# Second self-attention of a gated decoder kernel: fetch groups of four tiles, nine tiles ahead, with key products and weighted adds placed anew

## The reference, cut to what matters

```python
for l in range(L):                                   # L = 2
    x = x + _attn(_ln(x, ln1_w[l], ln1_b[l]), wq[l], wk[l], wv[l], wo[l], ...)   # 16 heads of 8, causal
    h = _ln(x, ln2_w[l], ln2_b[l])
    moe = _token_moe if l % 2 == 0 else _seq_moe
    x = x + moe(h, gate_w[l], gate_b[l], e_w1[l], e_b1[l], e_w2[l], e_b2[l])
# _token_moe: out = sum over 8 experts of _ffn(h, expert e) * cw[..., e], two of the cw are not zero (top 2)
# _ln: (x - mean) / sqrt(var + 1e-05) * w + b
```

## Time and profile before

| what | value |
|---|---|
| median of three runs | 1240.01 us |
| the profiled execution | 1244.81 us |
| its span, first to last instruction | 1243.1 us |
| PE busy | 1000.3 us (80%) |
| DVE busy | 834.7 us (67%) |
| ACT busy | 723.2 us (58%) |
| POOL busy | 587.8 us (47%) |
| mean granted TensorE clock | 0.857 |
| POOL's key products L658 (all three attentions) | x192, 242.4 us busy, 1284 ns each |
| DVE's maximum L1471 and subtraction L1474 | x96 each, 1215 and 1225 ns each |

### The profile page before, as it was taken

One profiled execution on the slowest core, in us unless ns is written; L12 is line 12 of the kernel. 1 busy time (PEld: TensorE's weight loads), 2 busy tenths in 40 slices (PEclk: granted clock), 3 DMA queues, 4 the chain that ended last, 5 costly groups with the idle time before them and its releaser, 6 DMA issues.

```text
span 1243.1 us, 30490 instructions
## 1 busy us (share of the span) xinstructions
PE 1000.3 (80%) x9835; PEld 772.5 (62%) x9835; DVE 834.7 (67%) x1980; ACT 723.2 (58%) x1821; POOL 587.8 (47%) x804
## 2 busy tenths in 40 slices
PE   4999988999974899996068799965999989899503
PEld 2677766677664899996036666754777769455301
DVE  4599998899866656664348897767222245499873
ACT  2577777878831077775055678843555532688543
POOL 6355545555640145553776765612334310478433
PEclk9899999999975599998577899965999995699855
DMA  4000040000011022222110004000000002011002
GB/s 126 11 15 15 15 140 2 2 1 0 1 39 29 11 58 63 67 64 50 52 27 20 20 8 135 1 1 0 1 0 0 0 19 59 11 45 46 27 0 68
DMA packets 51922, 38.77 MB, mean 31 GB/s; under 512 B 6073, under 2 KB 45477, under 8 KB 51861
## 3 DMA queue, kind: packets, MB, share of 16 engines
q1 hardware_dynamic: 46956, 28.88, 8.0%
q0 software_dynamic: 4320, 8.86, 2.8%
q10 hardware_dynamic: 584, 0.26, 0.1%
HBM read 29.13 MB, written 8.85 MB: 31 GB/s over the span
## 4 chain that ended last, share of the span: by engine, by line
PE 49%; DVE 14%; issue 11%; ACT 10%; POOLq 7%; POOL 3%; DMA 2%; SPq 1%; another core or an unknown queue 1%; DVEq 1%; ACTq 0%
PE ps_s L1036 9%; PE ps_o L1036 9%; PE ps_t L1120 7%; PE ps_v L1036 6%; PE ps_t L1036 6%; PE ps_a L1036 5%; POOLq L713 4%; ACT work L836 2%; POOL work L714 2%; DVE inner_all L1666 2%; PE ps_v L1140 1%; POOLq L703 1%; ACT vst L827 1%; DVE rowmax L1471 1%
## 5 line engine op out<-in xcount | busy, mean ns | idle before, releaser
L658 POOL TENSOR_TENSOR kbd<-kts,kmask 128x512 f32<-128x512 f32 x192 | 242.4, 1284 | 210.5 <-ACT qts L822 128.0
L844 ACT COPY probs_t<-ps_t 128x1024 f32<-128x1024 f32 x96 | 97.2, 1013 | 72.8 <-PE ps_t L1120 71.8
L678 POOL DMA_INDIRECT xg<-x_rows,row_from x71 | 73.8, 1039 | 137.6 <-DVE slot_of L1636 70.1
L1471 DVE TENSOR_REDUCE rowmax<-ps_s 128x16 f32<-128x1024 f32 x96 | 116.7, 1215 | 30.7 <-PE ps_s L1036 30.6
L1036 PE MATMUL ps_s<-kbd,qts 64*64 64x512 f32 (+1 forms) x1024 | 127.7, 571 | 0.2 <-issue 0.2
L1474 DVE TENSOR_TENSOR work<-ps_s,rowmax 128x1024 f32<-128x1024 f32 x96 | 117.6, 1225 | 3.3
L1036 PE MATMUL ps_o<-vst,probs_t 128*64 128x18 f32 x3072 | 110.4, 215 | 5.3 <-ACT probs_t L844 5.3
L1120 PE MATMUL ps_t<-ident,work 128*128 128x128 f32 x768 | 108.3, 287 | 7.3 <-ACT work L836 5.7
L1036 PEld LDWEIGHTS ps_o<-vst,probs_t 128*64 128x64 f32 x3072 | 100.8, 142 | 18.0 <-ACT probs_t L844 6.7
L836 ACT ACTIVATE work<-work 128x1024 f32<-128x1024 f32 x96 | 100.9, 1051 | 1.4 <-DVE work L1474 1.2
L1120 PEld LDWEIGHTS ps_t<-ident,work 128*128 128x128 f32 x768 | 91.1, 148 | 15.8 <-ACT work L836 15.7
(11 more groups left out here) (370 smaller groups left out, 2379.2 us busy)
## 6 DMA issues: line engine op xcount, KB each, us to landing
y_rows<-work SPq DMA_DIRECT2D x71, 64.0 KB
w<-in_L_ffn_e_w_dram SPq DMA_DIRECT2D x2, 2048.0 KB, 8.4
ctx_dup<-in_ctx_dram SPq DMA_DIRECT2D x64, 64.0 KB, 2.3
x_res<-in_x_dram SPq DMA_DIRECT2D x4, 512.0 KB, 6.6
ctx_in<-in_ctx_dram SPq DMA_DIRECT2D x32, 64.0 KB, 1.8
x_rows<-h_all SPq DMA_DIRECT2D x1, 2048.0 KB, 9.2
work<-in_ctx_dram SPq DMA_DIRECT2D x8, 256.0 KB, 2.8
out_dram<-work SPq DMA_DIRECT2D x16, 128.0 KB, 1.8
```

The source lines that it names most:

```text
L658: i = pool.tensor_tensor(km[:, par, g, :, :], kts[:, par, g:g + 1, :].to_broadcast([P, 8, SEQ]), kmask[:, :, :], ALU.mult)
L678: pool.indirect_dma_start(xg[:, t % XBUFS, :], None, x_d, bass.IndirectOffsetOnAxis(row_from[:, t:t + 1], 0)).then_inc(xg_loaded[t % XBUFS ...
L844: nc.scalar.copy(probs_t[:, par, :], ps_t[:, :]).then_inc(S["pts_ready"], 1)
L1471: V.tensor_reduce(rowmax[:, par, :], s3, AXX, ALU.max).then_inc(S["max_ready"], 1)
```

## The change

`GROUP` goes from 8 to 4. The attention runs `LEAD` = 7 iterations behind the fetches on DVE, the weighted adds `LAND` = 3, and on POOL the key product stands `AHEAD` = 9 tiles behind the fetch. POOL's key product of tile t also waits until the scores of tile t - 1 are done. The bias adds of four tiles become one instruction. On DVE the weighted adds and the fetched rows' statistics move from the end of the iteration to behind the subtraction, and the residual add to the end; the seven small instructions of a group become one `bn_aggr` per tile. On ACT the square root takes `EPS` as a bias and comes once in four tiles, now ahead of the attention's steps, which lose their lag.

```diff
-GROUP = 8
+GROUP = 4
 NGROUP = NT // GROUP
-LEAD = GROUP + 7
+LAND = 3
+LEAD = GROUP + LAND
+AHEAD = GROUP + 5
...
+                fresh(pool.memset(eps_col[:, :], EPS))
...
+            def four_biases(t, par):
+                if t % SUB == SUB - 1:
+                    pool.wait_ge(S["xn_ready"], SELF1 + t + 1)
+                    part = inner[:, (t + 1 - SUB) * D:(t + 1) * D].rearrange("p (a d) -> p a d", d=D)
+                    pool.tensor_tensor(part, part, obias[:, 1:2, :].to_broadcast([P, SUB, D]), ALU.add
+                                       ).then_inc(S["bias_added"], SUB)
+
+            def kbd_after_scores(t, par):
+                pool.wait_ge(S["scores_ready"], ATT[1] + t)
+                kbd_step(ATT[1])(t, par)
...
-            straight(later([(2, kbd_step(ATT[1])), (3, bias_step(1))], LEAD) + [(0, fetch)])
+            straight([(AHEAD, kbd_after_scores), (AHEAD - 1, four_biases), (0, fetch)])
...
-            straight(later(attention(1, 1), LEAD) + [(LEAD, normalise)],
-                     {GROUP * g + LEAD - 1: lambda g=g: row_std(CH_SELF1 + g, GROUP * g, GROUP * (g + 1))
-                      for g in range(NGROUP)})
+            def group_root(t, par):
+                if t % GROUP == 0:
+                    act.wait_ge(S["stats_done"], t + GROUP)
+                    nc.scalar.activation(stds[:, 0, t:t + GROUP], aggr[:, t:t + GROUP, 1], ACT.Sqrt, bias=eps_col[:, :]
+                                         ).then_inc(S["std_ready"], 1)
+
+            straight([(0, group_root)] + [step for step in attention(1, 1) if step] + [(0, normalise)])
...
-            hooks = {}
-            for g in range(NGROUP):
-                a, b = GROUP * g, GROUP * (g + 1)
-                hooks[a + LEAD - 1] = lambda k=CH_SELF1 + g, a=a, b=b: row_means(k, b, a, b, False, "stats_done")
-                hooks[a + LEAD] = lambda k=CH_SELF1 + g, a=a, b=b: row_rstd(k, a, b, False, True)
-            attend = attention(1, inner, inner, SELF1, rstd, 1.0)
-            straight(later([attend[0]] + attend[2:], LEAD)
-                     + [(4, combine_first), (5, combine_second), (6, sums_step(inner, "second_done", 0, "stats_done"))], hooks)
+            def fetched_stats(t, par):
+                dve.wait_ge(S["second_done"], t + 1)
+                V.bn_stats(stats[:, t, :], tile(inner, t)).then_inc(S["row_done"], 1)
+                dve.wait_ge(S["row_done"], t + 1)
+                V.bn_aggr(aggr[:, t, :], stats[:, t, :]).then_inc(S["stats_done"], 1)
+
+            def group_rstd(t, par):
+                if t % GROUP == 0:
+                    g, c = t // GROUP, slice(t, t + GROUP)
+                    dve.wait_ge(S["std_ready"], CH_SELF1 + g + 1)
+                    V.reciprocal(rstd[:, c], stds[:, 0, c]).then_inc(S["rstd_ready"], 1)
+                    dve.wait_ge(S["rstd_ready"], CH_SELF1 + g + 1)
+                    V.scalar_tensor_tensor(nbias[:, c].unsqueeze(2), aggr[:, c, 0:1], -1.0, rstd[:, c].unsqueeze(2),
+                                           ALU.mult, ALU.mult).then_inc(S["nbias_ready"], 1)
+
+            y_, _, shift_, sums_, add_ = attention(1, inner, inner, SELF1, rstd, 1.0)
+            straight(later([y_, shift_], LEAD) + [(LEAD, group_rstd), (LAND, combine_first), (LAND, combine_second)]
+                     + later([sums_], LEAD) + [(LAND, fetched_stats)] + later([add_], LEAD))
```

More of the change, by code:

```diff
@@ L246, in build @@
         half_gap = sb("half_gap", [P, NT])
+        aggr = sb("aggr", [P, NT, 2])
+        eps_col = sb("eps_col", [P, 1])
         var = sb("var", [P, NT])
@@ L381, in build @@
         csum_ps avec_ready adiag_ready a_ready d_ready ctil_ready qcopy_ready col_ready sum_ready cent_ready sqsum_ready gained negmd_ready emd_ready
-        vb16_ready gn_link square_ready gve_ready gstd_ready nbias_ready late_loaded x0_loaded x1_loaded x2_loaded x3_loaded inner_ready stats_done first_done second_done biased fin_link qb_ready amax_ready amrow_ps
+        vb16_ready gn_link square_ready gve_ready gstd_ready nbias_ready late_loaded x0_loaded x1_loaded x2_loaded x3_loaded inner_ready row_done stats_done first_done second_done biased fin_link qb_ready amax_ready amrow_ps
         amrow_done scale_ps scale_ready q8_ready q8t_ps q8t_ready acc8_ready o1_ready o3_ready xb_ready
@@ L662, in kbd_step, with bias_step @@
                 return fn
[L664 to L673, removed]
+            def bias_step(t, par):
+                pool.wait_ge(S["inner_ready"], t + 1)
+                pool.tensor_tensor(tile(inner, t), tile(inner, t), obias[:, 0, :], ALU.add
+                                   ).then_inc(S["bias_added"], 1)
+            def four_biases(t, par):
[7 more added lines that the diff above has]
+                kbd_step(ATT[1])(t, par)
             def gather(t):
@@ L689, in _ @@
             routing_constants()
-            chained(pool, [[(2, kbd_step(ATT["x"])), None], [(2, kbd_step(ATT[0])), (4, bias_step(0))]])
+            chained(pool, [[(2, kbd_step(ATT["x"])), None], [(2, kbd_step(ATT[0])), (4, bias_step)]])
             other_constants()
@@ L891, in row_std @@
             def row_std(k, a=0, b=NT, twice=False):
-                act.wait_ge(S["vare_ready"], k + 1)
+                act.wait_ge(S["vare_ready"], k + 1 - (NGROUP if k >= CH_PRE1 else 0))
                 n_ = 2 if twice else 1
@@ L1420, in row_means @@
             def row_means(k, need, a=0, b=NT, twice=False, done="bn_done"):
+                k -= NGROUP if k >= CH_PRE1 else 0
                 n = [STAT_LINKS * k]
```

## The result

The changed kernel takes **1196.8 us**, the median of four runs (1196.4 to 1198.2), against 1239.8 for the kernel before: ratio 0.967 (0.964 to 0.971). Run again beside the kernel before on another occasion it took 1198.9, ratio 0.968 (0.964 to 0.972).

A forecast was written before the change was run, and what follows sets the result against it. It saw POOL-only fetches first, then attention slowed by DVE collisions and low PE clock, then a PE-bound end. Start 16.1 plus middle 13.5 gave 29.6 us: 1244.8 to 1215.2, 1210.4 as median; range 1198 to 1230.

The forecast's parts named there:

- Start: Stage's start: fewer tiles fetched ahead and smaller first group move tile 1's key product from 633.22 to 617.1, 16.1 us earlier.
- rival A: Stage's start: ACT's unnamed waits don't come again, POOL alone sets tile 1 at 610.4; 6.7 us more, 1203.7; chance 0.15.
- the forecast's own case: Stage's start: ACT's whole start moves 16.1 us earlier with its unnamed waits kept, tile 1's product at 617.1; chance 0.62.
- the unnamed waits: ACT at the stage's start: first keys waited 9.01 us for something the trace does not name; forecast to stay.
- 22 intervals at 5.4: POOL beside the fetches: 22 intervals between key products from tile 1 on, 5.4 us each, 118.8 us.
- The low bound: POOL beside the fetches: 5.25 us a tile, POOL's own work alone, against 5.4 taken.
- Boundaries: ACT's extra square-root table loads: five group boundaries beside fetches at 0.6 us, 3.0; the sixth, in the PE-bound part, 3.0.
- Tail: Behind the fetches, PE-bound: 8 intervals between key products of 4.69 us each, 37.5 us.
- The stage's end: From the last key product to the stage's end: stays at 20.6 us.
- DVE's collisions: DVE's adds beside POOL's key products: hardly meet where the gate sets the start, meet about 1 us where fetches do.
- never 3: Sign of being right: DVE's add L1666 takes between 0.34 and 1.4 us and never 3.
- Rival C: PE idles at six boundaries and drops to 1.2 GHz, three tiles each at 8.54 us: +50, 1260; chance 0.06.

The follow-up runs named there:

- the reciprocal's move: Changed kernel with only the group's reciprocal and its product moved ahead of y, maximum and subtraction on DVE: 1239.4 us, ratio 0.997.
- adds last alone: Changed kernel with only the two weighted adds and the fetched rows' statistics put back to the end of DVE's iteration: 1209.4 us, ratio 0.976.

## Why the prediction was right, and where its sizes were off

- **Start: right, mis-sized by the trace.** Forecast 16.1, measured 23.5 against the trace that it was made from. Here rival A came true, with its chance of 0.15, and not the forecast's own case (tile 1's product where POOL alone puts it: 27.3 us behind the first fetch against 610.4 - 582.5 = 27.9; the forecast had 34.6). The change did not do away with the unnamed waits: the kernel before has them in one trace and not in the other. Like with like the term is 19.8, 8 tiles of fetches.
- **22 intervals at 5.4: 118.8 forecast, 116.1 measured.** The low bound (5.25, POOL alone) was nearly exact, 5.275. In the second trace of the changed kernel they take 118.4, since one product waits 2.45 us for the scores; so the forecast's 5.4 was as good a guess.
- **Boundaries: 3.0 forecast beside the fetches, nothing measured; 3.0 forecast behind them, 2.0 measured.** The first is the term that failed in size. Beside the fetches neither table load shows in an interval: the root is done before DVE asks for it, and PE, which waits 1.23 us for the exponential behind its load, has this to spare, because POOL sets the pace. Behind them PE sets the pace, and there the loads do show:

```profile
741.06 1.28 ACT L851 ACT_TABLE_LOAD   x1
742.10 2.50 POOL L664 TENSOR_TENSOR kbd<-kts,kmask 128x512 f32<-128x512 f32 x2 [2.79 <-PE ps_s L1056]
743.46 1.09 PE L1140 MATMUL ps_t<-ident,work 128*128 128x128 f32 x8 [1.23 <-ACT work L851]
748.23 1.28 POOL L664 TENSOR_TENSOR kbd<-kts,kmask 128x512 f32<-128x512 f32 x1 [2.40 <-PE ps_s L1056]
```

  From product to product this takes 6.13 us, and the interval before it, with the root's load (736.95), 5.29, against 4.69 each. A bias of four tiles stands in it too (744.56), but it isn't the reason: POOL waits 2.40 us behind it. With groups of eight a product with such a bias behind it (749.04) is followed by the next after 4.69 us:

```profile
751.49 1.28 POOL L681 TENSOR_TENSOR inner_all<-inner_all,obias 128x512 f32<-128x512 f32 x1
753.73 2.51 POOL L664 TENSOR_TENSOR kbd<-kts,kmask 128x512 f32<-128x512 f32 x2 [0.95 <-PE ps_s L1056]
```

  With POOL's product 17 tiles behind the fetch, three boundaries lie behind the fetches and each costs about the same 2.0; the two more of them take up what was to come back there. The Trainium skill ("ScalarE: Activation LUTs", section "What ACT_TABLE_LOAD costs") gives about 2.66 us for a switch, roughly half of it the load and the rest a drain. The trace has the load and no drain: the root follows 1.30 us behind the load's start (674.29, 675.59), as in the row of before.
- **Tail: 37.5 forecast, 39.4 measured** (727.51 to 766.91). The difference is the boundary just told, for which the forecast had its 3.0. The terms explain the middle: 162.3 - 2.7 (the 22 intervals) - 3.0 (boundaries beside the fetches) - 1.1 (tail and its boundary, 39.4 for 40.5) = 155.5.
- **The stage's end** was left at 20.6 and came to 16.4; 18.4 in the second trace of before (821.01 - 802.63), so some 2 us are the change's.
- **DVE's collisions.** "They do meet, for about 1 us" was too dear in the main: the adds stay at 0.34 to 0.71 in three tiles of four. But "never 3", a sign of being right, did not hold: the second add of tile 7, beside the very first product, takes 3.20, and the first add of tile 9, beside a product and a bias, 2.40. In the old order DVE's new list by itself gives 12.3 us, against 15.2 for all parts together.
- **Rival C is real, at another place.** Its price, a PE stall of over 3 us behind a boundary and tiles at 8.5 us after it, was right in kind (forecast 1260, the reciprocal's move measured 1239, with one interval of 10.5 to 11.8 per group and not three of 8.5). Its cause isn't the change of function alone: the 1.28 us of load is part of what DVE waits for, and the wait does harm because it stands ahead of `y`. I had not costed the place of the two small instructions at all, and with them in the wrong place the whole gain is lost.
- **The range** (1198 to 1230) ended 1.2 us above the median of 1196.8: A, the low POOL bound, boundaries at a third of their price and a stage's end shorter by 4.2 came together, and I had let it hold A and the low bounds only one at a time.

## What to carry to other kernels

Ask of every instruction what is queued behind it on its engine: a 0.2 us reciprocal ahead of the step that feeds TensorE cost some 40 us, because its wait of under 3 us became a stall, and the stall a stretch at half clock. Put work of the other stream (adds, statistics, a group's reciprocal) behind the step that TensorE waits for, and only then make the groups shorter: the same short groups gave 8 to 10 us in the new order and lost 5 (by the ratio) to 8 (by the medians) in the old. Price an unnamed wait from two traces of the same kernel, not from one.

## What the runs showed that I had not expected

**Late semaphores of TensorE.** In the first trace of before, and in three kernels of one occasion (groups of four in the old order, adds last alone, the reciprocal's move), the first keys wait 4.7 to 9.4 us on ACT for a projection whose recorded end is past (in the first trace of before it ends at 615.81 and the keys start at 623.30; in the second 616.02 and 616.07); in the fourth kernel of that occasion, groups of two, the second tile's wait 4.18. In the other eight experiments and in the changed kernel's first trace the first keys wait 1.6. Old and new order are on both sides, and on that occasion the kernel before took 1241.2 against 1236.1 and 1236.8 on the others. What causes it no run here shows.

**An add that started first still waited.** In the changed kernel's trace, DVE and POOL at the first product:

```profile
605.42 0.35 DVE L1681 SCALAR_TENSOR_TENSOR inner_all<-h_all,tw,inner_all 128x128 f32<-128x128 f32 x1 [1.18 <-DMA w<-y_rows,slot_of]
605.80 3.20 DVE L1687 SCALAR_TENSOR_TENSOR inner_all<-w,tw,inner_all 128x128 f32<-128x128 f32 x1
```

The product starts at 606.36, 0.56 us after the add, which needs 0.35 alone and ends only behind the product's two instructions (608.85), at 609.00. By the Trainium skill ("SBUF — State Buffer", section "Who interferes with whom") the second to issue is the one blocked; by these records it was the first, so a recorded start isn't the moment of issue to memory, or POOL's recorded start is late, or the rule doesn't hold here. The add at 697.23 above is the same case in the old order: it starts 0.17 us ahead of its product (697.40) and takes 3.24. No run tells the three apart.
